# Where the odd tile of thirteen stands: value tiles, context pieces and key chunks moved in a perceiver kernel

## What is computed

```
q = heads(query @ Wq.T + bq)            # 16 heads of 16
k = heads(bank @ Wk.T + bk)             # bank: the 1601 context rows of the batch
v = heads(bank @ Wv.T + bv)
attn = softmax(q / sqrt(16) @ k.T)
out = (attn @ v) @ Wo.T + bo
```

## Time and profile before

| | |
|---|---|
| median of three runs | 2087.93 us |
| profiled execution | 2091.72 us |
| its span, first to last instruction | 2089.8 us |
| mean granted TensorE clock | 0.985 of full |
| first scores of batch 0 start at | 94.3 us |
| batch 31's last scores start at | 2029.9 us |

### The profile page before, as it was taken

How to read it: one execution, slowest core, us unless ns; L and a number is a source line. 1 busy time by engine, 2 the same in 40 slices (tenths; PEclk the granted TensorE clock), 3 DMA queues, 4 the chain that set the end, 5 groups by cost and what they waited for, 6 DMA issues and landing times.

```text
span 2089.8 us, 72896 instructions
## 1 busy us (share of the span) xinstructions
PE 1965.7 (94%) x31852; PEld 1587.4 (76%) x31852; DVE 1288.1 (62%) x2276; ACT 1049.8 (50%) x1532; POOL 677.1 (32%) x1349
## 2 busy tenths in 40 slices
PE   6889989999999999999999999999999999999987
PEld 5667778877878787787878877787787777777764
DVE  2546656757666567666656676665666577565644
ACT  3345546555455555546555555564545444444441
POOL 4233342424333233333423333342433222233201
PEclk7899999999999999999999999999999999999999
DMA  5443433433523343434332524343243321222122
GB/s 172 163 149 102 150 115 123 149 121 111 165 91 133 112 151 107 141 125 146 106 125 93 172 88 146 119 136 122 95 139 97 120 88 63 79 71 89 50 73 71
DMA packets 124473, 243.92 MB, mean 117 GB/s; under 512 B 13953, under 2 KB 44801, under 8 KB 124161
## 3 DMA queue, kind: packets, MB, share of 16 engines
q1 hardware_dynamic: 123568, 239.23, 34.9%
q10 hardware_dynamic: 592, 0.04, 0.0%
HBM read 235.94 MB, written 3.15 MB: 114 GB/s over the span
## 4 chain that ended last, share of the span: by engine, by line
PE 77%; DVE 9%; ACT 7%; issue 5%; POOL 2%; DMA 0%; SPq 0%; POOLq 0%; DVEq 0%; ACTq 0%
PE M L820 12%; PE M L827 11%; PE SC L1039 10%; PE SC L1062 8%; PE O L1083 7%; PE X L877 5%; ACT probT L1285 4%; DVE mx L1636 3%; PE SC L1055 3%; PE M L877 3%; PE X L1149 2%; PE X L856 1%; PE M L922 1%; PE M L882 1%; PE X L1123 1%
## 5 line engine op out<-in xcount | busy, mean ns | idle before, releaser
L1636 DVE TENSOR_REDUCE mx<-SC 128x4 f32<-128x1600 f32 (+1 forms) x256 | 466.8, 1824 | 162.2 <-PE SC L1039 158.8
L1285 ACT ACTIVATE probT<-SC 128x2048 f32<-128x2048 f32 (+1 forms) x256 | 398.9, 1558 | 157.2 <-PE SC L1062 156.6
L660 POOL TENSOR_TENSOR rowsT<-raw,rowsT 128x256 fp32r<-128x256 f32 (+1 forms) x512 | 327.3, 671 | 362.2 <-ACT rowsT L1339 362.1
L827 PE MATMUL M<-wvs,rowsT 128*128 128x256 f32 x2496 | 357.5, 292 | 3.9 <-DVE PT L1618 1.7
L820 PE MATMUL M<-rowsT,wks 128*128 128x400 f32 (+1 forms) x1536 | 342.7, 364 | 6.8 <-POOL rowsT L660 1.3
L1226 ACT ACTIVATE kT<-M,bk 128x400 f32<-128x400 f32 (+1 forms) x256 | 151.7, 594 | 376.9 <-PE M L820 376.3
L820 PEld LDWEIGHTS M<-rowsT,wks 128*128 128x128 f32 x1536 | 272.5, 191 | 80.6 <-issue 64.0
L827 PEld LDWEIGHTS M<-wvs,rowsT 128*128 128x128 f32 x2496 | 313.7, 191 | 24.8 <-DVE PT L1618 2.9
L1432 DVE TENSOR_TENSOR V<-M,bv 128x512 f32<-128x512 f32 (+1 forms) x224 | 145.2, 648 | 256.5 <-PE M L827 251.3
L1039 PE MATMUL SC<-kT,bdq 32*128 32x400 f32 (+1 forms) x2048 | 246.4, 547 | 26.8 <-ACT probT L1285 22.9
L1083 PEld LDWEIGHTS O<-probT,V 128*17 128x17 f32 x13312 | 190.3, 98 | 67.7 <-issue 63.3
(11 more groups left out here) (283 smaller groups left out, 2455.0 us busy)
## 6 DMA issues: line engine op xcount, KB each, us to landing
ring<-in_ws_dram SPq DMA_DIRECT2D x428, 256.0 KB, 4.3
summed<-in_ctx_dram SPq DMA_DIRECT2D x60, 800.5 KB, 4.6
raw<-in_ctx_dram SPq DMA_DIRECT2D x64, 384.0 KB, 4.1
raw<-in_ctx_dram SPq DMA_DIRECT2D x32, 512.0 KB, 4.2
ring<-rounded_scratch SPq DMA_DIRECT2D x64, 256.0 KB, 3.7
raw<-in_ctx_dram SPq DMA_DIRECT2D x32, 321.0 KB, 4.7
out_dram<-x SPq DMA_DIRECT2D x16, 128.0 KB, 1.7
kT<-in_ctx_dram SPq DMA_DIRECT2D x2, 800.5 KB, 8.9
```

The lines of the kernel that those rows point to most:

```text
L660: ins = pool.tensor_tensor(rowsT[1][:, c, part], raw[:, c, part], rowsT[0][:, c, part], ALU.subtract)
L827: mm = pe.matmul(bank[:, (t - 2 * a) * D:(t - 2 * a + 1) * D], rowsT[xp][:, cc, t * P:(t + 1) * P], wvs[wp][:, cc, :], start=(at == cc == ...
L1285: act.activation(probT[step % 3][0:w, :, 0:len(ts), :].rearrange("p j t q -> p j (t q)"), SC[0:w, :, 0:len(ts) * P], ACT.Exp)\
L1636: dve.tensor_reduce(mx[c][:, :, n], SC[:, :, 0:KCH[n][1]], AX.X, ALU.max).then_inc(max_used, 1)
```

## The change

The tile that is alone among the values is tile 0 and no longer tile 12: value fill a covers tiles 2a - 1 and 2a (`tiles_of`), fill 0 is tile 0, and fill 6 covers tiles 11 and 12. So place 3 has one tile of values and place 2 two. Fills 2 and 3 change places (6 and 7), so that they run in order. The keys are cut at tile edges: 384, 384, 384 and 449. The pieces hold 3, 3, 3 and 4 tiles, and piece 0 and 1 name value fills as their last readers. "ff_in" moves from "B" to "C", from before the maxima to behind them. The weighted sums and VectorE's drain follow the new numbering.

```diff
-KCH = [(KEYS * n // NCH, KEYS * (n + 1) // NCH - KEYS * n // NCH) for n in range(NCH)]
+KCH = [(KEYS // P // NCH * n * P, (KEYS // P // NCH if n < NCH - 1 else KEYS // P - (NCH - 1) * (KEYS // P // NCH)) * P + (KEYS % P if n == NCH - 1 else 0)) for n in range(NCH)]
...
-        (11, "B"): "ff_in", (11, "D"): "ff0", (12, "B"): "ff1", (12, "D"): "ff2", (13, "B"): "fow", (14, "B"): "xq",
+        (11, "C"): "ff_in", (11, "D"): "ff0", (12, "B"): "ff1", (12, "D"): "ff2", (13, "B"): "fow", (14, "B"): "xq",
...
-FIRST = [[[value(4)], [value(5)], [value(6)], [value(0)], [key(0, 3)], [value(1)], [value(3)], [value(2)]],
-         [[value(4)], [value(5)], [value(6)], [value(0)], [key(0, 3)], [value(1)], [value(3)], [value(2)]]]
+FIRST = [[[value(4)], [value(5)], [value(6)], [value(0)], [key(0, 3)], [value(1)], [value(2)], [value(3)]],
+         [[value(4)], [value(5)], [value(6)], [value(0)], [key(0, 3)], [value(1)], [value(2)], [value(3)]]]
...
-PIECES = [(0, 4, key(1, 1)), (4, 7, key(1, 2)), (7, 10, value(4)), (10, KT, value(VF - 1))]
+PIECES = [(0, 3, value(2)), (3, 6, value(3)), (6, 9, value(4)), (9, KT, value(VF - 1))]
...
+def tiles_of(a):
+    return range(max(2 * a - 1, 0), 2 * a + 1)
...
-                        pe.wait_ge(low_ready, C * (len(PIECES) * n + piece_of(min(2 * a + 1, KT - 1)) + 1))
-                        for t in range(2 * a, min(2 * a + 2, KT)):
+                        pe.wait_ge(low_ready, C * (len(PIECES) * n + piece_of(2 * a) + 1))
+                        for n_, t in enumerate(tiles_of(a)):
...
-                                    mm = pe.matmul(bank[:, (t - 2 * a) * D:(t - 2 * a + 1) * D], rowsT[xp][:, cc, t * P:(t + 1) * P], wvs[wp][:, cc, :],
+                                    mm = pe.matmul(bank[:, n_ * D:(n_ + 1) * D], rowsT[xp][:, cc, t * P:(t + 1) * P], wvs[wp][:, cc, :],
...
-                            wait_drained(pe, (b, "value", ts[-1] // 2, 0))
+                            wait_drained(pe, (b, "value", (ts[-1] + 1) // 2, 0))
...
-                        m = min(2 * a + 2, KT) - 2 * a
+                        t0, m = tiles_of(a)[0], len(tiles_of(a))
...
-                        dve.tensor_tensor(values(n)[:, 2 * a * H:(2 * a + m) * H, 0:HD].rearrange("p (t h) e -> p t h e", t=m),
+                        dve.tensor_tensor(values(n)[:, t0 * H:(t0 + m) * H, 0:HD].rearrange("p (t h) e -> p t h e", t=m),
```

## The result

The changed kernel took 2095.59 us as the median of 22 runs (2091.08 to 2098.3). The kernel before took 2091.1 us in as many runs beside it (2084.75 to 2099.13). The ratio is 1.0019, with a 95% interval of 1.001 to 1.0028: slower, by little, but by more than the runs leave open. The profiled execution took 2094.98 us, its span is 2093.0 us, its mean granted clock 0.983 for 0.985. The forecast was 2086.7 us and a gain of 1.2. Some 3 us of that miss are the base: the median of the first three runs before, 2087.93, was low by chance.

What follows compares the result with a forecast made beforehand. TensorE, busy 94% of the span, was taken to bound the kernel. The terms +13.0 - 16.2 + 1 + 1 = -1.2 us gave 2090.5 us for the profiled execution and 2086.7 for the median, range 2077 to 2098.

Steps and rivals of the forecast that it cites:

- (a): Place 2 gets a value tile: 23.0 us gross, +13.0 us after the waits it fills.
- (b): Place 3 loses a value tile but can only shrink to the exponential's end: -16.2 us.
- (c): The 449-key chunk at places 1 and 5 lengthens reduction and maxima: +1 us, bounds +0.3 and +2.5.
- (d): The four-tile piece 3 delays the key fill at place 4 in batches 8 and 22, 0.56 us each: +1 us.
- The waits of the scores: At place 2, scores wait 0.2 to 0.3 us more for the reduction in six even batches.
- Rivals 1 and 2: 1 (0.09): VectorE keeps place 3's length, 2102.9 us; 2 (0.12): waits at place 2 hide its extra tile, 2079 us.
- Rival 3: Waits turn up elsewhere (piece 3's low part, ff0, the long reduction): +9 us, 2095; chance 0.13.
- the sum: Over the whole kernel, the terms for places 2 and 3, chunks and pieces add up to -1.2 us.

Runs made afterwards that it cites:

- e1_chunks: The kernel before with only the key chunks of 384, 384, 384 and 449; 2093.44 us, ratio 1.0023 to before.
- e3_values: The kernel before with only the new values and "ff_in", old chunks and pieces, but piece 2 split one place later; 2089.9 us, ratio 1.0007 to before.
- e9_hold: The changed kernel with idle matmuls: 24 in batch 3, 6 in batch 6, 12 in batch 15; 2097.74 us, ratio 1.0035 to before.
- e7_keep_all: The changed kernel with two idle matmuls in every value fill of place 3; 2095.45 us, ratio 1.0033 to before.
- s_after_minus: The changed kernel with 44 idle matmuls for 72 in TensorE's first wait; 2098.61 us, ratio 1.0035 to before.
- e6_values_keep: e3_values with 12 idle matmuls in batch 3 and 2 in batch 6; 2091.49 us, ratio 1.0001 to before.
- e5_keep_three: The changed kernel with 12, 2 and 12 idle matmuls in fills of batches 3, 6 and 15; 2092.14 us, ratio 1.0009 to before.
- e8_values_hold: e3_values with 24 idle matmuls in batch 3 and 6 in batch 6; 2089.78 us, ratio 1.0002 to before.

## Why the prediction was wrong

- **(a), (b), the mechanism:** right, and shown by the places. Place 3 gave 15.9 us for 16.2, place 2 took 8.4 for 13.0. The even batches took 5.6 of the 7.5 us counted there, the odd ones 2.8 of 5.5: the tile at place 2 fell into waits more often than I had counted.
- **(c):** +1 forecast; +1.5 to +2.8 by e1_chunks, at or a little above its upper bound of +2.5. **(d):** the key fill at place 4 waits in batches 8 and 22, for 1.53 us in batch 8, and each pays 0.9, not 0.56: the pass takes 2.78 us as forecast, but begins late.

```profile
619.29 2.78 POOL L664 TENSOR_TENSOR rowsT<-raw,rowsT 128x256 fp32r<-128x256 f32 x4
...
622.22 1.06 PE L824 MATMUL M<-rowsT,wks 128*128 128x450 f32 x4 [1.53 <-POOL rowsT L664]
```

- **The waits of the scores** for the reduction grew by 2.3 us in sum; at place 2 by 0.16 to 0.23 us in seven even batches, as said.
- **Rivals 1 and 2** have no place: place 3 did shrink, and place 2 did not stay as long as it was. Rival 3's number, 2095, was hit by another cause.
- **The step that failed** is the sum: "The profiled execution (2091.72 us, span 2089.8) would take 2090.5." It takes all that is not an instruction or a wait to be alike in both kernels. The clock is not. A moved tile was priced by its matmuls and waits alone, but in the changed order 3.41 us at place 3 of batches 6 and 15 run at 1.2 GHz, for 1.55 to 1.7 us each. Over the run the clock is 0.0038 lower, worth 4.7 us, and against a gain of about 1 from order and pauses it makes the loss of 3.4 by the means (2094.98 for 2091.58). The profile before showed the clock's row and a half-clock stretch at 288.9 us, and I read neither.
- That the changed order has these falls and the order before has not is shown by place for batches 6 and 15. That the waits cause them is not shown: e3_values and e9_hold have the fall in batch 6 without the wait of 0.45 us, e7_keep_all and s_after_minus have the waits without a fall. For the other half of the lost clock I know no fixed place: the falls vary from run to run, and the idle matmuls in e6_values_keep did not bring it back. Why the clock falls stays open.

No version beat the kernel before. e3_values, e5_keep_three, e6_values_keep and e8_values_hold equal it. The order of the new values with the old chunks is the best of all (rests of -4.4, -4.7 and -6.2 in three kernels), and each of the three lost it to clock and pauses.

## What to carry to other kernels

Where TensorE is busy for 94% of the time, a move of work between places has three prices: its instructions and waits, the clock, which can fall at a place that the move has changed, and the borders of 256 instructions, which every added or removed instruction shifts. Read the granted clock by place before and after. And before a change of a few us is believed, shift the stream by some idle matmuls in a wait: if that alone moves the time by more, medians don't rank two orders of work.

## Not expected of the hardware

- One pause for code costs up to 3.2 us, and TensorE goes on 1.2 to 1.6 us after the packet has landed. A shift of 56 instructions made the same work 13 us (0.6%) slower.
- A single 3.41 us stretch at 1.2 GHz comes at place 3 of batch 6 in ten of the twelve profiles with the new order of values, with the wait of 0.45 us ahead of it or without, and in none of the eight with the old order.
- The packet that ended the pause in batch 7 came while other transfers took 73% of the DMA engines; I did not try whether fewer transfers shorten it.
